# First attention layer of a two-layer kernel: three groups of transposes become one, in row halves of TensorE's array

## The reference

```python
xn = _ln(x, ln_w, ln_b)
q = xn @ Wq + bq
k = xn @ Wk + bk + (1.0 - src_mask) * -1000000.0
q = softmax(q.reshape(b, t, h, dh), axis=-1)      # over the features of a head
k = softmax(k.reshape(b, t, h, dh), axis=1)       # over the rows of a sequence
v = ((xn @ Wv + bv) * src_mask).reshape(b, t, h, dh)
att = einsum('bnhd,bnhl->bhdl', k, v)
y = einsum('bnhd,bhdl->bnhl', q, att).reshape(b, t, d)
scale, shift = split((silu(emb) @ W_emb + b_emb)[:, None, :], 2, axis=2)
return x + silu(_ln(y, ln2_w, ln2_b) * (1.0 + scale) + shift) @ W_out + b_out
```

## Time and profile before

| what | value |
|---|---|
| median of 3 runs | 2092.11 us (2091.98 to 2093.65) |
| profiled execution, its own time | 2092.2 us |
| its span, first to last instruction | 2090.3 us |
| PE busy | 2065.4 us, 99% |
| PE weight loads (PEld) busy | 1818.4 us, 87% |
| DVE busy | 1396.2 us, 67% |
| ACT busy | 1151.3 us, 55% |
| POOL busy | 579.0 us, 28% |
| DMA, mean over the span | 41 GB/s |

### The profile page before, as it was taken

The page is one execution under the profiler, slowest core; times in us unless marked ns, Lnnn a source line. Parts: engine busy times, 40 slices in busy tenths (PEclk is TensorE's granted clock), DMA queues, the critical chain, the costliest instruction groups (busy, mean ns, idle before and its releaser), DMA issues.

```text
span 2090.3 us, 48294 instructions
## 1 busy us (share of the span) xinstructions
PE 2065.4 (99%) x17499; PEld 1818.4 (87%) x17499; DVE 1396.2 (67%) x2995; ACT 1151.3 (55%) x3806; POOL 579.0 (28%) x861
## 2 busy tenths in 40 slices
PE   7999999999999999999999999999999999999997
PEld 5888888888888888888898989898898989898986
DVE  6877777777777777776665556665565655566655
ACT  4333333334323433354677777777777777777775
POOL 4323332333233322334222222222222222222220
PEclk9999999999999999999999999999999999999999
DMA  7211011100011001102210101101010101011000
GB/s 234 93 40 40 25 35 40 40 30 35 35 40 38 27 35 40 40 26 77 67 36 25 35 25 35 40 20 40 25 35 25 35 25 35 25 35 40 20 31 21
DMA packets 52165, 86.43 MB, mean 41 GB/s; under 512 B 5668, under 2 KB 14566, under 8 KB 52135
## 3 DMA queue, kind: packets, MB, share of 16 engines
q1 hardware_dynamic: 52118, 86.03, 12.1%
q10 hardware_dynamic: 16, 0.00, 0.0%
HBM read 52.32 MB, written 33.69 MB: 41 GB/s over the span
## 4 chain that ended last, share of the span: by engine, by line
PE 96%; DVE 2%; ACT 1%; DMA 0%; issue 0%; SPq 0%; POOL 0%; POOLq 0%; DVEq 0%; ACTq 0%
PE bank L538 14%; PE bank L539 14%; PE bank L540 14%; PE bank L547 9%; PE bank L548 9%; PE bank L549 9%; PE bank L1742 5%; PE bank L1755 3%; PE bank L1732 3%; PE bank L1129 3%; PE bank L1117 2%; PE bank L1014 1%; PE bank L1038 1%; PE bank L1692 1%; PE bank L1764 1%; PE bank L1042 1%
## 5 line engine op out<-in xcount | busy, mean ns | idle before, releaser
L547 PE MATMUL bank<-xT_hi,w_hi 128*128 128x256 f32 x1536 | 448.0, 292 | 0.8 <-DVE xT_lo L379 0.8
L548 PE MATMUL bank<-xT_lo,w_hi 128*128 128x256 f32 x1536 | 438.8, 286 | 0.0
L549 PE MATMUL bank<-xT_hi,w_lo 128*128 128x256 f32 x1536 | 436.1, 284 | 0.0
L1561 ACT ACTIVATE heads<-bank,top 128x128 f32<-128x128 f32 x1024 | 358.6, 404 | 88.1 <-DVE top L1354 87.9
L538 PE MATMUL bank<-w_hi,xT_hi 128*128 128x512 f32 x768 | 305.4, 398 | 0.4 <-DVE bias_all L396 0.4
L540 PE MATMUL bank<-w_lo,xT_hi 128*128 128x512 f32 x768 | 301.2, 392 | 0.0
L539 PE MATMUL bank<-w_hi,xT_lo 128*128 128x512 f32 x768 | 300.2, 391 | 0.0
L547 PEld LDWEIGHTS bank<-xT_hi,w_hi 128*128 128x128 f32 x1536 | 292.2, 190 | 8.6 <-issue 3.8
L548 PEld LDWEIGHTS bank<-xT_lo,w_hi 128*128 128x128 f32 x1536 | 292.4, 190 | 0.5 <-issue 0.5
L549 PEld LDWEIGHTS bank<-xT_hi,w_lo 128*128 128x128 f32 x1536 | 292.8, 191 | 0.0
L1354 DVE TENSOR_REDUCE top<-bank 128x4 f32<-128x512 f32 x256 | 162.8, 678 | 180.9 <-PE bank L1732 180.9
(11 more groups left out here) (203 smaller groups left out, 4048.6 us busy)
## 6 DMA issues: line engine op xcount, KB each, us to landing
xr<-in_x SPq DMA_DIRECT2D x32, 512.0 KB, 3.4
x_between_layers<-ends SPq DMA_DIRECT2D x64, 256.0 KB, 2.0
xr<-x_between_layers SPq DMA_DIRECT2D x32, 512.0 KB, 4.1
out<-ends SPq DMA_DIRECT2D x64, 256.0 KB, 2.1
store<-in_L_cond_W_emb SPq DMA_DIRECT2D x4, 1024.0 KB, 11.8
store<-in_L_cond_emb_w SPq DMA_DIRECT2D x3, 1024.0 KB, 8.0
mask_rows<-mask_parts SPq DMA_DIRECT2D x128, 2.0 KB
heads<-in_L_cond_Wk SPq DMA_DIRECT2D x1, 1024.0 KB, 7.6
```

The costliest lines, as they stand in the source:

```text
L547: yield nc.tensor.matmul(dst, w_hi[:, m, c, fs], a_hi[:, c], start=(first and c == 0), stop=False)
L548: yield nc.tensor.matmul(dst, w_hi[:, m, c, fs], a_lo[:, c], start=False, stop=False)
L549: yield nc.tensor.matmul(dst, w_lo[:, m, c, fs], a_hi[:, c], start=False, stop=(last and c == C - 1))
L1561: last = nc.scalar.activation(prob[:, a, c, :], ps[a][:, c * P:(c + 1) * P], ACT.Exp, bias=top[:, b, h:h + 1], accum_out=total[:, b, h:h + 1])
```

## The change

The 8 key blocks, 8 query blocks and 8 blocks of the next x are turned by it in one group behind the values. The semaphores that were waited for here and there in between are now awaited ahead of the last value matmul:

```diff
-            for b in range(PAIR):
-                run(project_rows(nc, w_hi, w_lo, V, xT_hi, xT_lo, b, ps[4 + b], C)).then_inc(s["v_ps"], 1)
+            run(project_rows(nc, w_hi, w_lo, V, xT_hi, xT_lo, 0, ps[4], C)).then_inc(s["v_ps"], 1)
+            value_steps = project_rows(nc, w_hi, w_lo, V, xT_hi, xT_lo, 1, ps[5], C)
+            run(islice(value_steps, 3 * C - 1))
             pe.wait_ge(s["k_exp"], seq(2, i, 2))
-            pe.wait_ge(s["q_less"], seq(PAIR, i, PAIR))
+            pe.wait_ge(s["q_exp"], seq(PAIR, i, PAIR))
+            if not first:
+                pe.wait_ge(s["g"], seq(PAIR, i - 1, PAIR))
             if not last:
-
-                x_transposed(i + 1)
+                pe.wait_ge(s["xn"], seq(PAIR, i + 1, PAIR))
+            run(value_steps).then_inc(s["v_ps"], 1)
+            keys_turned()
+            queries_turned()
+            if not last:
+                x_turned()
             else:
                 next(following)
+            pe.wait_ge(s["v"], seq(PAIR, i, PAIR))
             if first:
-                run(emb.products(pe, ps[0]))
+                run(emb.products(pe, ps[O_BANKS[0]]))
             else:
-                run(out_rows(i - 1, 0, 0))
-            weights_turned(i, 0)
-            weights_turned(i, 1)
-            outputs1 = () if first else out_rows(i - 1, 1, 1)
-            run(islice(outputs1, 7))
-
+                run(out_rows(i - 1, 0, O_BANKS[0]))
+
+            pe.wait_ge(s["k_rows"], seq(2, i, 2))
             for b in range(PAIR):
                 if b == 1 and not last:
-                    pe.wait_ge(s["xT_lo"], seq(PAIR, i + 1, PAIR))
+                    pe.wait_ge(s["xT_lo"], seq(2, i + 1, 2))
...
-            run(outputs1)
+            pe.wait_ge(s["qT"], seq(2, i, 2))
             if first:
-                emb.turned(pe, ps[1])
-
-            for b in range(PAIR):
-                banks = ((4, 5), (6, 7))[b]
+                emb.turned(pe, ps[O_BANKS[1]])
+            else:
+                run(out_rows(i - 1, 1, O_BANKS[1]))
+
+            for b in range(PAIR):
+                banks = Y_BANKS[b]
```

Banks are given out anew:

```diff
-    A_BANKS = (6, 2)
+    HALF = P // 2
+    A_BANKS, O_BANKS, Y_BANKS = (6, 2), (4, 0), ((5, 1), (6, 7))
+    X_BANKS, KEY_BANKS, QUERY_BANKS = (2, 3), (6, 7), (0, 1)
```

The operations that read the transposes (`x_low`, `key_rows`, `x_high`, `query_T`) are as many and as large as before, but each takes one half of 64 rows for both b, strided, in place of one b; `x_high` waits for both halves at once. Two orders change:

```diff
 # VectorE
             query_shift(i, 0)
...
-            query_shift(i, 1)
-            if not first:
-                end_silus(i - 1)
             if not last:
                 norm(i + 1, (i + 1) % RING)
             else:
                 next(following)
+            query_shift(i, 1)
+            if not first:
+                end_silus(i - 1)
             values(i, 0)
             values(i, 1)
+            key_rows(i)
             if not last:
-                x_low(i + 1, (ps[2], ps[3]))
+                x_low(i + 1)
...
-            key_rows(i, 0)
-            key_rows(i, 1)
             weights_of(i)
 # ScalarE
+            query_T(i)
             if not last:
-                x_high(i + 1, (ps[2], ps[3]))
+                x_high(i + 1)
             else:
                 next(following)
-            query_T(i)
```

More of the change, by code:

```diff
@@ L549, in project_features @@
         yield nc.tensor.matmul(dst, w_lo[:, m, c, fs], a_hi[:, c], start=False, stop=(last and c == C - 1))
+def turn_halves(nc, ident, banks, blocks):
+    half = P // 2
+    for n, src in enumerate(blocks):
+        for r in range(2):
+            rows = slice(half * r, half * r + half)
+            last = nc.tensor.transpose(banks[r][:, half * n:half * n + half], src[rows, :], ident[rows, rows],
+                                       tile_position=(half * r, 0))
+    return last
 def run(steps):
@@ L767, in norm, with x_low @@
                                         ALU.mult).then_inc(s["xn"], 1)
-        def x_low(pair, banks):
-            for b in range(PAIR):
-                dve.wait_ge(s["xT_hi"], seq(PAIR, pair, b + 1))
-                nc.vector.tensor_tensor(xT_lo[:, :, b, :], banks[b][:, :].rearrange("p (c t) -> p c t", c=C),
-                                        f32(xT_hi[:, :, b, :]), ALU.subtract).then_inc(s["xT_lo"], 1)
+        def x_low(pair):
+            for r in range(2):
+                rows = slice(HALF * r, HALF * r + HALF)
+                dve.wait_ge(s["xT_hi"], seq(2, pair, r + 1))
+                nc.vector.tensor_tensor(xT_lo[:, :, :, rows],
+                                        ps[X_BANKS[r]][:, :].rearrange("p (c b t) -> p c b t", c=C, b=PAIR),
+                                        f32(xT_hi[:, :, :, rows]), ALU.subtract).then_inc(s["xT_lo"], 1)
         def end_norm(prev):
@@ L818, in values, with key_rows @@
                                            ALU.mult, ALU.add).then_inc(s["v"], 1)
[L820 to L823, removed]
+        def key_rows(i):
+            dve.wait_ge(s["k_tr"], seq(1, i, 1))
+            for r in range(2):
+                nc.vector.tensor_copy(k_rows[:, :, :, HALF * r:HALF * r + HALF],
+                                      ps[KEY_BANKS[r]][:, :].rearrange("p (b c t) -> p b c t", b=PAIR, c=C))\
+                    .then_inc(s["k_rows"], 1)
         def weights_of(i):
@@ L890, in body @@
             if first:
-                emb.copy_rows(dve, ps[0])
+                emb.copy_rows(dve, ps[O_BANKS[0]])
             else:
-                end_add(i - 1, (i - 1) % RING, 0, 0)
-            key_rows(i, 0)
-            key_rows(i, 1)
+                end_add(i - 1, (i - 1) % RING, 0, O_BANKS[0])
             weights_of(i)
             if first:
-                emb.leave_bank(dve, ps[1])
+                emb.leave_bank(dve, ps[O_BANKS[1]])
             else:
-                end_add(i - 1, (i - 1) % RING, 1, 1)
+                end_add(i - 1, (i - 1) % RING, 1, O_BANKS[1])
             outputs(i)
@@ L921, in _, with x_high @@
     def _(act):
-        def x_high(pair, banks):
-            for b in range(PAIR):
-                act.wait_ge(s["xT_ps"], seq(PAIR, pair, b + 1))
-                nc.scalar.activation(xT_hi[:, :, b, :], banks[b][:, :].rearrange("p (c t) -> p c t", c=C),
+        def x_high(pair):
+            act.wait_ge(s["xT_ps"], seq(PAIR, pair, PAIR))
+            for r in range(2):
+                nc.scalar.activation(xT_hi[:, :, :, HALF * r:HALF * r + HALF],
+                                     ps[X_BANKS[r]][:, :].rearrange("p (c b t) -> p c b t", c=C, b=PAIR),
                                      ACT.Copy).then_inc(s["xT_hi"], 1)
@@ L962, in query_T @@
         def query_T(i):
-            for b in range(PAIR):
-                act.wait_ge(s["q_tr"], seq(PAIR, i, b + 1))
-                nc.scalar.activation(qT[:, b], ps[(6, 4)[b]][:, :].rearrange("p (c t) -> p c t", c=C),
+            act.wait_ge(s["q_tr"], seq(1, i, 1))
+            for r in range(2):
+                nc.scalar.activation(qT[:, :, :, HALF * r:HALF * r + HALF],
+                                     ps[QUERY_BANKS[r]][:, :].rearrange("p (b c t) -> p b c t", b=PAIR, c=C),
                                      ACT.Copy).then_inc(s["qT"], 1)
@@ L1007, in _, with x_turned @@
         following = second["tensor"](pe)
[L1009 to L1015, removed]
+        def x_turned():
+            banks = [ps[n] for n in X_BANKS]
+            turn_halves(nc, ident, banks, [xn[:, b, c * P:(c + 1) * P] for c in range(C) for b in range(PAIR)])\
+                .then_inc(s["xT_ps"], PAIR)
         def z_transposed(prev):
@@ L1031, in out_rows, with keys_turned, queries_turned @@
             done.then_inc(s["o_ps"], 1)
[L1033 to L1043, removed]
+        def keys_turned():
+            banks = [ps[n] for n in KEY_BANKS]
+            turn_halves(nc, ident, banks, [k_exp[:, c, b, :] for b in range(PAIR) for c in range(C)])\
+                .then_inc(s["k_tr"], 1)
+        def queries_turned():
+            banks = [ps[n] for n in QUERY_BANKS]
+            turn_halves(nc, ident, banks, [q_exp[:, b, c * P:(c + 1) * P] for b in range(PAIR) for c in range(C)])\
+                .then_inc(s["q_tr"], 1)
         def body(i, first, more, last):
@@ L1070, in body @@
                     continue
-                if f == 2:
+                if f == 0:
                     pe.wait_ge(emb.s["scale"], 1)
+                if f == 2 and not first:
+                    pe.wait_ge(s["y"], seq(PAIR, i - 1, 1))
                 keys(f)
```

5 lines of the change are left out of this document (1 added, 4 removed).

## The result

The changed kernel takes 2058.01 us (median of 4 runs, 2057.49 to 2059.18) against 2092.05 us: a ratio of 0.9835, 95% interval 0.9822 to 0.9848. The forecast was 2060.3 us in a range of 2054 to 2076, so 34.0 us went where 31.9 were forecast. The profiled executions have spans of 2056.2 and 2090.3 us.

A forecast was written before the change was run, and what follows sets the result against it. The prediction took the length of the TensorE (PE) stream, busy 99% of the span, as the bound. Savings of 29.7 + 0.4 + 1.75 = 31.9 us from 2092.2 gave 2060.3 us, range 2054 to 2076.

The forecast's parts named there:

- The pair: Layer 0 transposes: each 128x128 block becomes two half-row transposes, 0.060 us a pair, bounds 0.055 and 0.072; 24 pairs, 1.44 us.
- A: Rival: the halves don't overlap, their two loads going one after the other; 0.124 us a pair, 2108 us; chance 0.09.
- B: Rival: a load of 128 columns takes longer than the moving half; 0.110 us a pair, about 2097 us; chance 0.04.
- The two more changes of form: PE's array going into halves and out again once more an iteration: 0.34 us, bounds 0.25 and 0.50.
- The group: Pairs plus changes of form in a middle iteration: 1.44 + 0.34 = 1.78 us against 2.77.
- rival C: PE waits ahead of att for x low parts or another link, strided half copies running longer: 2075 us; chance 0.12.
- The longest chain: ACT's query and x copies, then DVE's second low part near 401.8; second batch's att wants it about 402.5: 0.7 us left.
- The norm: Next xn moves into DVE's idle 1.49 us, where two operations take 1.00 us; it hides with 0.5 us left.
- PE wants x1 at 407.8: End of an iteration: the add of output 1 ends at 407.1, and PE wants x1 at 407.8.
- The middle iterations: 30 iterations of the first layer save 0.99 us each, 29.7 us in all.
- The term of 1.75 us: Iteration 31: query and key transposes go into output projection 0's wait for h_lo, saving 1.75 us, bounds 1.0 and 1.75.
- Iteration 0: The gain is cut, as the first key block now waits for the embedding's small DVE operations: 0.4 us, between 0 and 0.99.

The follow-up runs named there:

- norm late: Changed kernel with the next x normalised where it was before, behind the second query shift and the silus on VectorE: 2084.2 us.
- x1 late: Changed kernel with one more unread VectorE reduction of 0.68 us ahead of the add that gives the second x1: 2073.8 us.
- less load: Changed kernel with only 64 columns of weights loaded for each half of a key block, 64 moving columns as before: 2054.9 us.
- last pair's version: Changed kernel, but in layer 0's last pair VectorE normalises layer 1's first x behind the silus, as before: 2059.4 us, then 2059.2 us.
- less moving: Changed kernel with key blocks turned by 32 rows of each half only, so 32 moving columns in place of 64: 2063.3 us.
- before with norm early: Kernel before with the next x normalised ahead of the second query shift on VectorE, except in the last pair: 2088.4 us.

## Why the prediction was right

**The pair.** Taken at 0.060 us, measured 0.062. The halves do overlap, rivals A and B fell, and the row that was nearest was the opening's 64-row transposes (0.062), not the mean with att. The reason given was half right: I had the moving side as the bound that falls; it falls below the load, which then decides.

**The two more changes of form.** Taken at 0.34 us from att; measured 0.35 in the changed kernel and 0.37 when a round trip was added once more. The group costs 1.84 us, not 1.78.

**The covers.** No link of rival C held. The longest chain had 0.95 us left where 0.7 was forecast, since ACT's four copies took 2.1 us and not 2.4. The norm fits its gap, as forecast; the run with the norm late shows that it was worth 25 us, and that this order is a condition of the gain rather than a part beside it.

**What was missed, the start of the keys.** The step "PE wants x1 at 407.8" is wrong: PE wants it half a microsecond earlier, since the branch of its loop stands behind that wait. The kernel before lost 0.11 us there each of the 28 times that the loop goes back, 3.1 us in all, and no term of the sum had it. The middle iterations beat the forecast by 2.3 us: they lost 0.06 each in the group and gained these 0.11 at x1, and pair 1 gained 0.7 more than the others, most of it the wait for xn that was in its timeline and that I took to be 0.15 as in the others.

**The last pair.** The term of 1.75 us measured 1.09, and 1.65 (36.33 less 34.68) with the order of before, so that the transposes alone are worth nearly what was forecast. Its step said that the transposes don't touch the h_lo on which PE waits. They don't, but the moved norm does: beside POOL's low weights two xn take 2.95 us, the second query shift, its exponential, ACT's next high part and h_lo follow later. I had checked the norm's gap in a middle iteration only.

**Iteration 0** came to the 0.4 us that was forecast. Layer 1's 0.56 us is luck: it is the stretch of lower clock in the last 17 us, and two profiles of the changed kernel differ by as much there, 1107.3 and 1106.7 us.

So the total owes part of its nearness to luck: 0.06 x 30 too much for the group and 0.66 for the last pair, against 3.1 + 0.7 too little for x1 and pair 1 and 0.56 that isn't the change's.

## What to carry to other kernels

Transposes of f32 that stand together can go in row halves and start nearly twice as often (0.062 us apart and not 0.109), but this pays only in groups large enough for one more change of the array's form, here by the sum above more than eight blocks. Such a group wants everything at once, so what feeds it must be moved forward on the other engines in the same change, and checked in the first and last iterations too, where those engines do other work. A wait at the end of a loop body should be judged by the branch behind it: a semaphore that comes in time for the matmul can be late for the branch.

## What the runs showed of the hardware

**The branch.** From the end of the x1 add to the first key load it is 0.50 us in the kernel before (408.27 to 408.77), and 0.6 us to the first key matmul with x1 late, in a PE program with one register step, a branch of 0.21 us and another register step between (with x1 late also a step on a semaphore). Over the 28 turns of the loop the first is 0.50 to 0.54 us. Where the branch isn't taken it is a record of 0.08 us, and the next matmul starts 0.29 us behind x1. The view of waits shows nothing of it until PE runs dry, and then only as "issue".

**Two row forms.** Tiles of 32 rows beside tiles of 64 rows cost about 0.14 us at the border, though both are row tiles. A border between loads of 64 and of 128 columns, both of 64 rows, cost nothing: with less load the first query pair starts 0.056 us behind the last key pair (384.297, 384.353).

**When the clock rises.** In the opening TensorE's full clock, 2.4 GHz, is granted 14 to 16 us after the start in some profiled executions and only at 19.7 to 21.1 us in others, with the same work ahead of it; until then it is the lower level, 1.2 GHz. The timelines of PE at 16 us, of the last pair's version and of the changed kernel timed once more:

```profile
16.44 0.41 PE L548 MATMUL bank<-xT_lo,w_hi 128*128 128x256 f32 x1
16.65 0.41 PE L549 MATMUL bank<-xT_hi,w_lo 128*128 128x256 f32 x1
```

```profile
16.30 0.28 PE L548 MATMUL bank<-xT_lo,w_hi 128*128 128x256 f32 x1
16.42 0.28 PE L549 MATMUL bank<-xT_hi,w_lo 128*128 128x256 f32 x1
```

0.21 us a step against 0.12. The profiles in which it rises late (norm late, x1 late, less moving, before with norm early, last pair's version both times) have the keys of pair 1 some 1.8 to 2.3 us later than the kernel that they were made from. At the end of every profile the lower level comes once more, for 6.8 or 10.2 us. The runs of one kernel lie in clusters one to two us apart, the kernel before at 2091.9 to 2092.4 and 2093.3 to 2094.6 in one series. That the clock makes these clusters isn't shown, since only one execution in each run was profiled. So the periods above, and not the medians, decide where a few us are at stake. What makes the clock rise early or late is open.
